# A feed-forward head of 21 dense units, roots taken within scatters, two banks for batch 0's turns, router weights kept

## The reference

```
x = x + 0.5 * moe(layernorm(x))      # 16 experts, top 4
x = x + attention(layernorm(x))      # 16 heads of 16, causal
x = x + 0.5 * moe(layernorm(x))      # the same weights again

def moe(x):
    probs = softmax(x @ gate_w.T);  w, idx = top_k(probs, 4);  w = w / sum(w)
    scores = sum over k of w[k] * one_hot(idx[k])
    expert_out = (silu(x @ w1[e]) * (x @ w3[e])) @ w2[e]        # 256 -> 128 -> 256
    return sum over e of scores[e] * expert_out[e]
```

## Time and profile before

| | us | share of the span |
|---|---|---|
| median of three runs | 1627.24 | |
| the profiled execution, its own time | 1627.28 | |
| its span | 1625.3 | |
| TensorE busy (PE) | 1441.6 | 89% |
| VectorE busy (DVE) | 1031.7 | 63% |
| ScalarE busy (ACT) | 778.8 | 48% |
| GpSimd busy (POOL) | 635.2 | 39% |

### The profile page before, as it was taken

One profiled execution on the slowest core, in us unless ns is written; L12 is line 12 of the kernel. 1 busy time (PEld: TensorE's weight loads), 2 busy tenths in 40 slices (PEclk: granted clock), 3 DMA queues, 4 the chain that ended last, 5 costly groups with the idle time before them and its releaser, 6 DMA issues. The chain is left out here.

```text
span 1625.3 us, 32606 instructions
## 1 busy us (share of the span) xinstructions
PE 1441.6 (89%) x10022; PEld 983.2 (60%) x10022; DVE 1031.7 (63%) x2384; ACT 778.8 (48%) x1316; POOL 635.2 (39%) x676
## 2 busy tenths in 40 slices
PE   3877999999978779999999999999569699999998
PEld 2656888888857633444344344343257588888887
DVE  4564545365778768887788778783457264635666
ACT  3402566554115523665566566567351255655511
POOL 2371434765604460222122222223235325176752
PEclk9988999999989967999999999999678799999999
DMA  7551656886314930342234342200222236588852
GB/s 265 189 207 53 195 182 213 264 240 203 90 36 127 233 108 1 55 67 41 41 41 67 41 54 41 41 2 2 66 74 78 75 124 218 172 263 245 248 162 75
DMA packets 159249, 199.06 MB, mean 122 GB/s; under 512 B 18196, under 2 KB 132472, under 8 KB 159096
## 3 DMA queue, kind: packets, MB, share of 16 engines
q1 hardware_dynamic: 140664, 146.69, 34.4%
q0 software_dynamic: 18432, 50.36, 9.4%
HBM read 105.22 MB, written 91.49 MB: 121 GB/s over the span
## 5 line engine op out<-in xcount | busy, mean ns | idle before, releaser
L1560 ACT ACTIVATE attn_prob<-attn_b_ps 128x1024 f32<-128x1024 f32 (+3 forms) x352 | 304.1, 870 | 219.2 <-PE attn_b_ps L1728 217.3
L1606 DVE TENSOR_REDUCE attn_max_a<-attn_a_ps 128x1 f32<-128x512 f32 (+3 forms) x432 | 279.2, 669 | 72.6 <-PE attn_a_ps L1711 40.6
L464 POOL DMA_INDIRECT xs_dram<-ffn_xn,ffn_index x192 | 188.3, 981 | 245.5 <-DVE ffn_index L736 188.8
L1708 PE MATMUL attn_a_ps<-k_rows,q_rows 96*128 96x512 bf16 (+3 forms) x768 | 250.3, 349 | 21.2 <-DVEq L1598 7.5
L478 POOL DMA_INDIRECT ffn_gathered<-ys_dram,ffn_index x192 | 195.5, 1018 | 97.6 <-issue 55.7
L1504 POOL TENSOR_SCALAR_AFFINE_SELECT attn_prob<-attn_prob 128x512 f32<-128x512 f32 x128 | 81.1, 635 | 363.1 <-ACT attn_prob L1560 360.5
L780 DVE TENSOR_TENSOR ffn_xs_lo<-ffn_xt_ps,ffn_xs_hi 128x512 fp32r<-128x512 f32 x144 | 97.8, 679 | 160.4 <-ACT ffn_xs_hi L552 159.6
L1752 PE MATMUL attn_o_ps<-attn_prob,attn_v_now 128*17 128x256 f32 (+1 forms) x2560 | 187.4, 366 | 0.0
L1728 PE MATMUL attn_b_ps<-q_rows,k_rows 98*128 98x512 bf16 (+3 forms) x768 | 185.9, 330 | 0.3 <-ACT attn_prob L1560 0.3
L1708 PEld LDWEIGHTS attn_a_ps<-k_rows,q_rows 96*128 96x128 bf16 x768 | 75.2, 98 | 179.9 <-DVE attn_max_a L1606 103.5
L184 PE MATMUL ffn_gu_ps<-ffn_w_hi,ffn_xs_hi 128*128 x564 | 170.3, 302 | 2.1 <-DVE ffn_xs_lo L780 2.1
(11 more groups left out here) (190 smaller groups left out, 2711.9 us busy)
## 6 DMA issues: line engine op xcount, KB each, us to landing
ffn_xs<-xs_dram SPq DMA_DIRECT2D x138, 256.0 KB, 3.5
ys_dram<-ffn_y SPq DMA_DIRECT2D x138, 256.0 KB
xs_dram<-ffn_y SPq DMA_DIRECT2D x16, 768.0 KB, 10.8
qk_parts<-proj_cut SPq DMA_DIRECT2D x32, 384.0 KB, 3.1
k_rows<-qk_parts SPq DMA_DIRECT2D x96, 128.0 KB, 4.5
q_rows<-qk_parts SPq DMA_DIRECT2D x96, 128.0 KB, 6.7
ffn_w_stage<-in_L_ffn_w_dram SPq DMA_DIRECT2D x64, 128.0 KB, 2.5
x_res<-in_L_attn_x_dram SPq DMA_DIRECT2D x4, 1024.0 KB, 8.2
```

What stands on the lines that cost most here:

```text
L464: pool.indirect_dma_start(xs_dram[(b + 1) % 2], bass.IndirectOffsetOnAxis(index[:, b, i, k:k + 1], 0), xn[:, b % 2, i, :], None, bounds_ch ...
L1560: act.activation(prob[PROB[kt]][:, h:h + heads, prob_at(kt, kt * P):prob_at(kt, S)], b_ps[:, slot, :].rearrange("p (h t) -> p h t", h=head ...
L1606: dve.tensor_reduce(dst, a_ps[:, bank, 0:heads * keys].rearrange("p (h k) -> p h k", h=heads), AX.X, ALU.max).then_inc(a_free, 1)
L1708: ins = pe.matmul(a_ps[:, bank, i * keys:end], q_rows[q][0:SROWS, h0 + i, qt * P:(qt + 1) * P], k_rows[q][0:SROWS, h0 + i, first:first + k ...
```

## The change

- `HEAD` and `TAIL` are now 21 and 11 units: units 16 to 20, the first five of chunk 1, move from the tail to the head. The parts that counted on 16 count on `HEAD` where they mean the head's end.
- Batch 1's front begins in unit 1 instead of unit 0 (`FIRST` 2, offsets from 4 on), batch 2's in unit 13 instead of 8, so that it stands as before against the head's end. In the slots nothing moves.
- `square_root(2)` is issued within `scatter(1)`, ahead of its last tile (4 of 32 DMAs), and `square_root(3)` within `scatter(2)`, ahead of its last two tiles (8 of 32).
- The eight turns of batch 0 alternate between the banks `f_ps` and `at_ps`, and each is issued one ahead of the logits of the tile before; the logits of batch 0 go to a part of `y_ps`. Unit 0 waits for the low parts of four tiles, not eight; the wait for the other four stands at unit 16. The wait for the router of batch 0 (`shift_ready`) moves from batch 1's first turn to the first `dense_down`.
- On VectorE batch 1's statistics stand in one piece behind the fourth low part, not in two pieces behind the second and the fourth.
- `gate_t` is allocated once for both blocks; the load, the turn and the copy of the router weights are done in the first block alone.
- Combines of batch 3 start in iteration 3 of the tail instead of 4; with 11 units in the tail and the last pair in iterations 11 and 12, that pair is added behind the last dense unit.

```
+HEAD, TAIL = 21, 11
+ROOT_AT = {1: 7, 2: 6}
-FIRST, SECOND, THIRD = 4, 8, 14
-COMBINE = {1: (47, 50, 54, 57), 2: (61, 64, 68, 71), 3: (4, 6, 8, 11)}
+FIRST, SECOND, THIRD = 2, 13, 14
+COMBINE = {1: (47, 50, 54, 57), 2: (61, 64, 68, 71), 3: (3, 6, 8, 11)}
...
         def head_offsets(e):
-            offsets = [(1, o) for o in (FIRST + 2 * e, FIRST + 2 * e + 1) if o < OFFSETS]
+            offsets = [(1, o) for o in (FIRST + 2 * e, FIRST + 2 * e + 1) if 4 <= o < OFFSETS]
...
-            for b, begin in ((2, SECOND - E - 2), (3, THIRD)):
+            for b, begin in ((2, SECOND - HEAD - 2), (3, THIRD)):
...
+        def turned_at(b, i):
+            return at_ps if b == 0 and i % 2 else f_ps
+
+        def logits_at(b):
+            return f_ps[:, 2 * P:3 * P] if b else y_ps[:, 0, 0, 0:P]
...
             if x_in is not None:
                 load_x(0)
-            sp.dma_start(gate_rows[:, :], gate_w).then_inc(gate_loaded, 16)
+                sp.dma_start(gate_rows[:, :], gate_w).then_inc(gate_loaded, 16)
...
                 for i in range(BT):
+                    if i == ROOT_AT.get(b):
+                        square_root(b + 1)
                     for k in range(TOP_K):
                         pool.indirect_dma_start(xs_dram[(b + 1) % 2], ...
...
             scatter(1)
-            square_root(2)
             scatter(2)
-            square_root(3)
             scatter(3)
...
             for i in range(BT):
                 cut_dense(i)
-                if i == 1:
+                if i == 3:
                     early_stats(1)
-                if i == 3:
                     late_stats(1)
...
-            for e in range(E):
-                dense_gate(E + e)
-                if e:
-                    add_dense(E + e - 1, 0)
-                    add_dense(E + e - 1, 1)
+            for e in range(TAIL + 2):
+                if e < TAIL:
+                    dense_gate(HEAD + e)
+                if 0 < e <= TAIL:
+                    add_dense(HEAD + e - 1, 0)
+                    add_dense(HEAD + e - 1, 1)
                 for late in range(2):
                     if e - late in COMBINE[3]:
                         combine(3, 2 * COMBINE[3].index(e - late), late)
-            add_dense(2 * E - 1, 0)
-            add_dense(2 * E - 1, 1)
...
             def turn(b, i):
                 if i == 0 and b >= 2:
                     pe.wait_ge(prefix_taken, b - 1)
-                elif i == 0 and b == 1:
-                    pe.wait_ge(shift_ready, 1)
                 pe.wait_ge(xn_ready, b * BT + i + 1)
+                if b == 0 and i >= 2:
+                    pe.wait_ge(xt_ready, i - 1)
...
+                    if k == E:
+                        pe.wait_ge(x_lo_ready, BT)
...
+                elif j == 0:
+                    pe.wait_ge(shift_ready, 1)
...
+            turn(0, 0)
             for i in range(BT):
-                turn(0, i)
+                if i + 1 < BT:
+                    turn(0, i + 1)
                 logits(0, i)
-            pe.wait_ge(x_lo_ready, BT)
-            for e in range(E):
+            pe.wait_ge(x_lo_ready, CHUNK_TILES)
+            for e in range(HEAD):
```

More of the change, by code:

```diff
@@ L191, in tiles_of, with ffn @@
     return 1 if n % PAIRS == PAIRS - 1 and SLOT_TILES % 2 else 2
-def ffn(nc, name, nth, scattered, row_gathered, x_in, x_res, ident, before_b, ones_b, gate_w, w1, w3, w2, xs_dram, ys_dram, out):
+def ffn(nc, name, nth, scattered, row_gathered, gate_t, x_in, x_res, ident, before_b, ones_b, gate_w, w1, w3, w2, xs_dram, ys_dram, out):
     with ExitStack() as ctx:
@@ L621, in _ @@
                     copy_y(n - 1)
-            for e in range(E):
-                dense_gate(E + e)
+            for e in range(TAIL):
+                dense_gate(HEAD + e)
         @block.vector
@@ L671, in router @@
                 dve.wait_ge(logit_ready, (b + 1) * BT)
-                steps.then(dve.tensor_copy(logit[:, :, :], f_ps[:, 2 * P:3 * P].rearrange("p (i e) -> p i e", e=E)))
+                steps.then(dve.tensor_copy(logit[:, :, :], logits_at(b).rearrange("p (i e) -> p i e", e=E)))
                 for i in range(BT):
@@ L815, in _ @@
             inverse_root(0)
-            dve.wait_ge(gate_turned, 1)
-            dve.tensor_copy(gate_t[:, :, :], f_ps[:, 0:KT * E].rearrange("p (h e) -> p h e", h=KT)).then_inc(gate_ready, 1)
+            if x_in is not None:
+                dve.wait_ge(gate_turned, 1)
+                dve.tensor_copy(gate_t[:, :, :], y_ps[:, 1, 0, 0:KT * E].rearrange("p (h e) -> p h e", h=KT)).then_inc(gate_ready, 1)
             for i in range(BT):
                 cut_dense(i)
-                if i == 1:
+                if i == 3:
                     early_stats(1)
-                if i == 3:
                     late_stats(1)
@@ L840, in _ @@
                     front(b, o)
-            add_dense(E - 1, 0)
-            add_dense(E - 1, 1)
+            add_dense(HEAD - 1, 0)
+            add_dense(HEAD - 1, 1)
             for n in range(-2, N + 1):
@@ L879, in logits @@
                 for h in range(KT):
-                    ins = pe.matmul(f_ps[:, 2 * P + i * E:2 * P + (i + 1) * E], xt[:, i % 2, h, :], gate_t[:, h, :],
+                    ins = pe.matmul(logits_at(b)[:, i * E:(i + 1) * E], xt[:, i % 2, h, :], gate_t[:, h, :],
                                     start=(h == 0), stop=(h == KT - 1))
@@ L980, in down @@
                 ins.then_inc(y_ready, 1)
[L982 to L986, removed]
+            if x_in is not None:
+                pe.wait_ge(gate_loaded, 16)
+                for h in range(KT):
+                    ins = pe.transpose(y_ps[:, 1, 0, h * E:(h + 1) * E], gate_rows[:, h * P:(h + 1) * P], ident[0:E, 0:E])
+                ins.then_inc(gate_turned, 1)
+                pe.wait_ge(gate_ready, 1)
+            turn(0, 0)
             for i in range(BT):
-                turn(0, i)
+                if i + 1 < BT:
+                    turn(0, i + 1)
                 logits(0, i)
-            pe.wait_ge(x_lo_ready, BT)
-            for e in range(E):
+            pe.wait_ge(x_lo_ready, CHUNK_TILES)
+            for e in range(HEAD):
                 offsets = head_offsets(e)
@@ L1006, in _ @@
                     dense_down(e - 1, 1)
-            dense_down(E - 1, 0)
-            dense_down(E - 1, 1)
+            dense_down(HEAD - 1, 0)
+            dense_down(HEAD - 1, 1)
             used = {}
@@ L1026, in _ @@
                     down(n - 1, used.pop(n - 1))
-            for e in range(E):
-                dense_up(E + e, 0)
-                dense_up(E + e, 1)
+            for e in range(TAIL):
+                dense_up(HEAD + e, 0)
+                dense_up(HEAD + e, 1)
                 if e:
-                    dense_down(E + e - 1, 0)
-                    dense_down(E + e - 1, 1)
+                    dense_down(HEAD + e - 1, 0)
+                    dense_down(HEAD + e - 1, 1)
             dense_down(2 * E - 1, 0)
@@ L1884, in program @@
         x_res = sb("x_res", [P, TILES, D], F32)
+        gate_t = sb("gate_t", [P, KT, E], F32)
         ident = sb("ident", [P, P], F32)
@@ L1895, in program @@
         ys_dram = [nc.dram_tensor(f"ys_dram{b}", [SLOT_TILES * P, D], F32, kind="Internal").ap() for b in range(BLOCKS)]
-        last = ffn(nc, "ffn1", 0, scattered, row_gathered, x, x_res, ident, before_b, ones_b, gate_w, w1, w3, w2, xs_dram, ys_dram, None)
+        last = ffn(nc, "ffn1", 0, scattered, row_gathered, gate_t, x, x_res, ident, before_b, ones_b, gate_w, w1, w3, w2, xs_dram, ys_dram, None)
         with ExitStack() as norm_ctx, ExitStack() as attn_ctx:
@@ L1903, in program @@
             attention(nc, x_res, v_res, ident, ident_b, mask_qk, wo, bo, rows)
-        ffn(nc, "ffn2", 1, scattered, row_gathered, None, x_res, ident, before_b, ones_b, gate_w, w1, w3, w2, xs_dram, ys_dram, out)
+        ffn(nc, "ffn2", 1, scattered, row_gathered, gate_t, None, x_res, ident, before_b, ones_b, gate_w, w1, w3, w2, xs_dram, ys_dram, out)
 _INS = ["L0_attn_x", "L0_attn_WQ", "L0_attn_bQ", "L0_attn_WK", "L0_attn_bK", "L0_attn_WV", "L0_attn_bV",
```

14 lines of the change are left out of this document (7 added, 7 removed).

## The result

The changed kernel takes **1575.38 us** (median of four runs, 1573.09 to 1581.26) against 1627.39 of the kernel before (also a median of four): a ratio of 0.969, 95% interval 0.9666 to 0.9713. The direction, the order of size and most terms held, but the kernel gained more than the sum says. The profiled execution took 1581.26, its span is 1579.5.

The account below looks back on a forecast made before the run. It took an ordering stall in the heads, TensorE waiting behind GpSimd's scatters, and TensorE-bound tails as the bound. Heads +1.7, slots -2.4, tails -38.4, end +1.3 give -37.8 from 1627.3: 1590 us, range 1577 to 1604.

Parts of the forecast that it names:

- The ordering stall: In each head batch 2's root queues behind GpSimd's 32 scatters; TensorE waits 14.5 us (15.2 first block), then 2.25 of slow clock.
- the gap of 2.2: At unit 17 in the head, TensorE still waits 2.2 us for batch 2's first turn, bounds 0 and 4.5.
- The start's lead: At each head's start, two banks and unit 0 before batch 1 save 6.7 us: 2.2 and a hidden unit of 4.5.
- rival 1: At each head's start, unit 0 only pushes batch 1's turns back; lead 2.2, each head +4.5 us: 1599, chance 0.13.
- The tails: Each tail of 11 units: -22.5 us, with +3.3 for combines behind the last dense add; -19.2 each.
- the kept weights: In the second block's head, dropping the router weights' load, turns and copy gains nothing, as they are hidden.
- Rival 2: In the tails, gathers hold the end if both waits for a combine stay, 2 x 5.8 us: 1602, chance 0.10.
- Rivals 3 and 4: In the heads, 28 scatters stretch to 1.8 us each (1598, chance 0.04), or far enough to be slower (0.03).
- the sum of the head: Head: +22.5 - 14.5 - 2.25 - 6.7 + 2.2 = +1.2 us in the second block, +0.5 in the first.
- That collision: In the head, VectorE's scale of batch 1 takes 2.21 us while GpSimd subtracts weights; it moves along, no gain.
- The ends: Behind the last dense add: combines +3.3 us in each block, and a second store +1.3 in the second block.
- the low bound: Whole kernel: all favourable bounds of start, gap, slots, second store and hidden unit together, 1576.4 us, rounded to 1577.

Follow-up runs that it names:

- first4: The changed kernel with batch 1's front one unit earlier (`FIRST` 4 in place of 2), as before the change: 1591.22 us.
- one_bank: The changed kernel with all turns of batch 0 in one bank, each behind the logits of the tile before: 1581.14 us.
- cuts_late: The changed kernel with ScalarE's high parts of the weights, and so GpSimd's subtractions, one unit later: 1582.66 us.
- root_alone: The kernel before with only batch 2's root moved behind 20 scatters of batch 1 and batch 3's behind 24 of batch 2: 1591.87 us.
- roots_behind: The changed kernel with the roots of batches 2 and 3 behind all 32 scatters again: 1579.77 us.

## Why the prediction was right and wrong

*Right.* The ordering stall and its size: the waits of 14.5 and 15.2 and the slow clock behind them are gone. With the roots alone moved the heads fall by 15.1 and 16.1, where the sum has 15.25 and 14.55 (15.2 and 14.5, and 2.25 of slow clock, less the gap of 2.2). The gap left at unit 17 is 1.71 (2.2 forecast). The start's lead is one unit and 2.1 in the first head, 3.8 in the second, by ScalarE's silus of unit 4 before and unit 5 after (2.2 and a unit forecast); first4 and one_bank show both parts, and rival 1 falls. The tails and the kept weights came as priced. Rival 2 shows at its edge, 0.65 of waiting for a gather. Rivals 3 and 4 fall: the scatters stayed at 1.28 us each.

*Wrong.* The step that failed is the sum of the head: it has no term for the unit in which batch 1's rows are placed. Of the collisions between batch 1's front and GpSimd's subtractions I looked at one, the scale held for 2.21 us, and wrote "That collision moves along and I give it no gain". For the scale this is true (2.25 and 2.24 after). What failed is to let it stand for all of them, as if the front and the subtractions were one block. The front moves a unit; the subtractions hang on ScalarE's weight cuts, unit by unit, and stay. So the 10.4 to 10.5 us ahead of unit 7's silu, one of the two longest pitches beside the stall, were put at no change without a reason. This unit gave back 4.3 and 4.2, and the one behind it 0.3 and 0.5: 9.3 of the 11.9 by which the heads were missed. cuts_late and first4 show the cause, for 2.2 to 2.8 of a unit; the rest goes with the granted clock, which after like waits stayed up in one head of root_alone (8.40) and fell in the other (10.52). What decides between the two is open. Most of what remains of the 11.9 is the second head's start, 1.6 above its term, and the units of the stall, 0.5 and 0.9 shorter than summed; no run takes these apart. I had also turned the rule of the Trainium skill, SBUF — State Buffer, section "SBUF: two separate sides", only one way, VectorE against GpSimd's descriptors, where GpSimd's arithmetic against VectorE was the case.

*Also.* The ends were short by 1.8 and 0.8: the combines take 3.24 as forecast, but the attention's first statistics come 3.2 behind them, not 1.25, and in the second block 0.65 of waiting for a gather comes on top. What holds the attention's start back is open. And 6 us between the profiled execution and the median are scatter, for which the low bound had no room (its sum was 1576.4, rounded up to 1577); by the first profile alone the time lies within the range.

*Not asked.* I priced the five units as filling the gap (-14.5) and never asked whether the root alone would close it. Either of the two closes it, as root_alone and roots_behind show; with the root moved the five units are a loss of 10.

## What to carry to other kernels

When one engine's work moves by a step, list what does not move with it: each instruction of the moved part meets a new neighbour on the other engines, for better or worse. A held instruction shows in no wait; look for rows whose duration is many times that of the same form elsewhere, and price the longest unit pitches one by one, before and after. When a stall is an order, try the order alone before filling the stall with work.

## What was not expected of the hardware

VectorE's instructions with two SBUF inputs ended with GpSimd's subtraction, whichever came next: `ffn_base` (2.36 and 2.43 us), `ffn_row` (1.98) or `ffn_chosen` (2.45), where 0.29 is usual, and `ffn_shift` (2.35), where 0.17 is. The one exception in these profiles is an `ffn_shift` of the kernel before that began 0.03 behind the subtraction and took its 0.17. VectorE's adds from PSUM (0.88 for two) and, beside a busy VectorE, GpSimd's scatters (1.28 each) went on undisturbed. After like waits of TensorE, 1.5 to 1.75 and then 1.63, a unit took 8.4 us with the granted clock at 1.00 and 10.3 to 10.5 with 0.70 to 0.73.
